# Four transposes of two-byte data moved from TensorE to transposing DMAs on SyncE, in a decoder layer on one core

## The reference, cut to what matters

```
1. x = LN(x + [x + rec + bit_linear(silu(bit_linear(rms(rec), w_gate)), w_down)])
     with h = rms(x); a = sigmoid(bit_linear(h, w_a) + bias); i, v alike;
     rec[t] = a[t] * rec[t-1] + sqrt(1 - a^2) * i * v          (a scan over tokens)
     bit_linear(h, w): each token of h is scaled to +-127 and rounded, w is rounded to -1, 0, 1
2. x = LN(x + attention(x, ctx))      16 heads of 16, rotary embedding, softmax over 256 keys
3. x = LN(x + s2 * relu2(s1 * relu2(s0 * [x, -x] @ k0) @ k1) @ k2)      k entries are +-1
```

## Time and profile before

| | |
|---|---|
| median of three runs | 956.42 us |
| profiled execution | 957.39 us, of which 955.6 us are the span from the first to the last instruction |
| PE busy | 832.9 us (87%) |
| DVE busy | 689.7 us (72%) |
| ACT busy | 544.1 us (57%) |
| POOL busy | 300.1 us (31%) |
| chain that ended last | PE 47%, DVE 22%, DMA 10%, ACT 9%, issue 7% |
| granted TensorE clock | mean 0.97, full in nearly all of the span after the first tenth |

### The profile page before, as it was taken

The page is one execution under the profiler, slowest core; times in us unless marked ns, Lnnn a source line. Parts: engine busy times, 40 slices in busy tenths (PEclk is TensorE's granted clock), DMA queues, the critical chain, the costliest instruction groups (busy, mean ns, idle before and its releaser), DMA issues.

```text
span 955.6 us, 17622 instructions
## 1 busy us (share of the span) xinstructions
PE 832.9 (87%) x6750; PEld 629.4 (66%) x6750; DVE 689.7 (72%) x1249; ACT 544.1 (57%) x909; POOL 300.1 (31%) x483
## 2 busy tenths in 40 slices
PE   1557789999999999999989999999999999997876
PEld 1233457786777777686867677676867677775655
DVE  8566578686969787786869696886869697866332
ACT  2453756657484747657574747566574747472331
POOL 5331415142423315151433334051424334141001
PEclk9876799999999999999999999999999999999999
DMA  8033160707052441707061532607070524325000
GB/s 277 0 59 53 45 79 16 108 13 117 8 101 34 71 64 41 94 13 122 14 106 17 90 46 52 83 27 108 14 114 10 101 34 62 62 38 75 1 12 22
DMA packets 98323, 57.43 MB, mean 60 GB/s; under 512 B 7841, under 2 KB 97473, under 8 KB 98241
## 3 DMA queue, kind: packets, MB, share of 16 engines
q1 hardware_dynamic: 98240, 56.31, 35.7%
HBM read 39.24 MB, written 16.79 MB: 59 GB/s over the span
## 4 chain that ended last, share of the span: by engine, by line
PE 47%; DVE 22%; DMA 10%; ACT 9%; issue 7%; POOL 2%; SPq 2%; DVEq 0%; ACTq 0%; POOLq 0%
PE bankC L1006 12%; PE bankA L816 11%; PE bankC L991 6%; DMA out<-x 6%; PE bankA L942 5%; PE slotB L910 3%; PE slotB L929 3%; PE bankA L807 3%; DMA q_st<-m_lo 3%; DVE x L1234 3%; DVE bn L1226 2%; DVE st L1204 2%; DVE nmax L1283 2%; ACT L666 2%; POOL rstd L534 2%
## 5 line engine op out<-in xcount | busy, mean ns | idle before, releaser
L1006 PE MATMUL bankC<-h0h,w 128*128 128x256 f16 x1024 | 233.4, 273 | 6.7 <-DVE h0l L1327 6.7
L1006 PE MATMUL bankC<-h0l,w 128*128 128x256 f16 x1024 | 232.9, 273 | 0.0
L1283 DVE TENSOR_REDUCE nmax<-slotB 128x4 f32<-128x1024 f32 x128 | 153.2, 1218 | 7.5 <-PE slotB L910 6.7
L716 ACT ACTIVATE pr<-slotB 128x1024 f32<-128x1024 f32 x128 | 129.3, 1025 | 37.6 <-PE slotB L929 37.4
L1006 PEld LDWEIGHTS bankC<-h0h,w 128*128 128x128 f16 x1024 | 100.5, 98 | 22.7 <-issue 9.8
L1006 PEld LDWEIGHTS bankC<-h0l,w 128*128 128x128 f16 x1024 | 100.4, 98 | 11.9
L533 POOL TENSOR_SCALAR rstd<-mv 128x2 f32<-128x2 f32 x48 | 9.3, 193 | 295.6 <-DVE mv L1229 295.6
L910 PE MATMUL slotB<-k_st,q_st 97*128 97x256 bf16 x512 | 78.9, 279 | 8.1 <-issue 5.1
L929 PE MATMUL slotB<-q_st,k_st 99*128 99x256 bf16 x512 | 75.9, 276 | 8.4 <-DMA q_st<-m_lo 4.8
L498 POOL TENSOR_SCALAR st<-st 128x2 f32<-128x2 f32 x32 | 7.7, 240 | 230.9 <-ACT junk L658 194.1
L1327 DVE SCALAR_TENSOR_TENSOR h1l<-bankC,h1h 128x512 f16<-128x512 f32 x64 | 43.6, 682 | 41.9 <-ACT h1h L741 41.9
(11 more groups left out here) (197 smaller groups left out, 1789.5 us busy)
## 6 DMA issues: line engine op xcount, KB each, us to landing
k_st<-scr SPq DMA_DIRECT2D x96, 128.0 KB, 5.2
q_st<-scr SPq DMA_DIRECT2D x96, 128.0 KB, 4.9
scr<-kpart SPq DMA_DIRECT2D x16, 384.0 KB, 3.6
scr<-qpart SPq DMA_DIRECT2D x16, 384.0 KB, 3.7
x<-in_x SPq DMA_DIRECT2D x16, 256.0 KB, 2.9
cT<-in_ctxT SPq DMA_DIRECT2D x16, 256.0 KB, 2.9
out<-x SPq DMA_DIRECT2D x16, 256.0 KB, 5.3
pr<-in_k SPq DMA_DIRECT2D x1, 1024.0 KB, 10.2
```

The source lines that it names most:

```text
L716: act.activation(pr[i % 2][:, c, :, :].rearrange("p h s -> p (h s)"), slotB[ringB.slot(g, name)][:, :], ACT.Exp, scale=DH ** -0.5).then_in ...
L1006: ins = pe.matmul(bankC[ringC.slot(g, name)][:, e * T:(e + 1) * T], w_1[:, i // 2, (2 * m + e) * P:(2 * m + e + 1) * P], (h0h, h0l)[i % 2] ...
L1283: dve.tensor_reduce(nmax[:, hg * HG * NT + n:(hg + 1) * HG * NT:NT], slotB[ringB.slot(g, name)][:, :].rearrange("p (h s) -> p h s", s=S), ...
```

## The change: what it does

For `xqT`, `rqT` and the gate, DVE's `round_tokens` gets one more pass: it takes `ROUND` off again and writes a bf16 copy (`xq`, `rq`, `gq`) with tokens on partitions. For `x2`, ACT and DVE now form the high and the low part before the transpose, side by side in one tile `x2p`. Then SP issues one transposing DMA each, SBUF to SBUF: `xqT` and `rqT` move 128 KB (four 128x128 blocks of two-byte numbers), the gate (`sqT`) and `x2T` 256 KB (eight blocks). PE's transposes for these, ACT's drains with `neg_round` and the PSUM slots of all four are gone. The projections wait for the DMA's semaphore and read the tile by token block. POOL's `scale` now waits for `round2` of the group before, and `gate` on ACT for its `round3`, since both reuse a source tile.

```diff
+            def across(src, dst, arrived):
+                sp.dma_start_transpose(dst, src).then_inc(arrived.sem, 16)
...
+            def sqT_(g):
+                if g >= 1:
+                    sp.wait_ge(*ringA.filled(g - 1, "down"))
+                sp.wait_ge(*q3.at(g))
+                across(flat(gq), sqT[:, :, :, :].rearrange("p n c t -> p (n c) t"), sqT_in)
+
+            def x2T_(g):
+                if g >= 1:
+                    sp.wait_ge(*ringC.filled(g - 1, f"l0_{KT // 2 - 1}"))
+                sp.wait_ge(*xl_s.at(g))
+                across(x2p[:, :, :, :].rearrange("p a n d -> p (a n d)"),
+                       x2T[:, :, :, :, :].rearrange("p a n c t -> p (a n c) t"), x2T_in)
...
-            def unround(g, name, dst):
-                act.wait_ge(*ringA.filled(g, name))
-                act.activation(dst, bankA[ringA.slot(g, name)][:, :], ACT.Identity, bias=neg_round)\
-                   .then_inc(ringA.free_sem(g, name), 1)
...
-            def sqT_(g, k):
-                if k == 0:
-                    pe.wait_ge(*q3.at(g))
-                transposed(g, f"sqT{k}", sg[:, :, 2 * k * P:(2 * k + 2) * P])
...
-            def round_tokens(g, src, factor, done):
+            def round_tokens(g, src, factor, dst, gone, done):
                 for n in range(NT):
-                    ins = dve.tensor_scalar(src[:, n, :], src[:, n, :], factor[:, n:n + 1], ROUND, ALU.mult, ALU.add)
-                ins.then_inc(done.sem, 1)
+                    own.mark(dve.tensor_scalar(src[:, n, :], src[:, n, :], factor[:, n:n + 1], ROUND, ALU.mult, ALU.add))
+                own.settle()
+                if g >= 1:
+                    dve.wait_ge(*gone.at(g - 1))
+                dve.tensor_scalar(dst[:, :, :], src[:, :, :], -ROUND, None, ALU.add).then_inc(done.sem, 1)
...
-                dve.tensor_tensor(flat(xl), slotB[ringB.slot(g, "x2T")][:, 0:512], flat(xh), ALU.subtract)\
-                   .then_inc(ringB.free_sem(g, "x2T"), 1)
+                dve.tensor_tensor(x2p[:, 1], x2[g % 2][:, :, :], x2p[:, 0], ALU.subtract).then_inc(xl_s.sem, 1)
```

More of the change, by code:

```diff
@@ L52 @@
 TIMES = """
[L53 to L72, removed]
@@ L73 @@
-    l1_3.0 P169.46 | l1_3.1 P171.66 | l1_3.2 P173.27 | l1_3.3 P173.89 A182.97 V185.57 | l2.0 P184.84 | l2.1 P190.11
-    l2.2 P190.5 | l2.3 P192.35 V196.85 | bn3 V233.28 G247.94 | out A239.18 | store S228.22
+    w:s V-358.73 P-345.58 | w:m V-255.03 A-334.52 P-294.13 | w:a V8.56 | w:iv V27.56 | w:g1 V8.92 P-141.16
+    w:g2 V21.1 A4.94 P17.85 | w:gate V32.32 | w:down V46.74 | w:bv P16.86 A27.81 | w:bias P39.65 V67.73
+    w:mask V23.89 S22.86 | w:sgn V32.42 | w:k0 V49.53 | w:k2 V60.27 | w:k1.0 A46.61 | w:k1.1 A66.03 | w:k1.2 A101.24
@@ new lines @@
+    w:k1.3 A112.84 | w:rbk G27.13 | loadx S75.98 | loadc S133.66 | scale A0 G5.04 V3.65 | stat1 G17.5 | round V9.79
+    xqT S18.34 | iv0 P29.33 A30.86 V33.66 | iv1 P31.53 A33.54 V32.75 | a P14.91 A23.29 | aT P27.95 A29.67
+    sq A33.67 | ivT P36.5 V34.38 | cum V34.64 | recur V37.33 | rec P42.81 A41.36 V44.61 | max2 V44.95 | stat2 G46.07
+    round2 V45.93 | rqT S64.43 | gate0 P54.85 A53.74 V54.83 | gate1 P55.41 A57.91 V56.09 | stat3 G58.47
+    round3 V56.51 | sqT S70.13 | down P61.75 V63.26 | bn V65.59 G77.42 | x1 V72.53 | kv0 P39.4 A40.55
@@ new lines @@
+    kv1 P41.46 A52.41 | rotk G52.22 | krT P58.53 A59.58 V62.77 G73.84 | kput S70.68 | kget S71.73
+    x1T P64.24 A71.82 | xb G92.01 | q P64.9 V78.72 | rotq G87.46 V80.29 | qrT P79.22 A81.89 V81.33 | qput S89.05
+    qget S95.74 | score0 P95.11 V92.1 | score1 P95.72 V94.03 | score2 P97.32 V97.13 | score3 P98.97 V97.95
+    score4 P100.72 V102.44 | score5 P104.92 V103.12 | score6 P107.79 V103.73 | score7 P108.58 V106.7
+    max P110.48 A111.55 V109.12 | maxrow S122.37 | exp0.0 P112.75 A114.43 | exp0.1 P112.95 A114.63 | pv0 P116.67
@@ new lines @@
+    exp1.0 P114.08 A114.91 | exp1.1 P115.58 A116.83 | pv1 P117.18 A126.19 | exp2.0 P116.79 A116.99
+    exp2.1 P117.13 A123.31 | pv2 P119.99 | exp3.0 P117.84 A126.73 | exp3.1 P117.9 A129.42 | pv3 P122.17 A134.14
+    oTok P124.27 V133.79 | oT P135.45 A135.88 | wo P136.57 V137.96 | bn2 V138.37 G151.09 | x2 V140.72
+    x2T A144.38 V141.09 S169.48 | l0_0 P150.05 A152.72 V147.7 | l0_1 P150.24 A155.3 V149.72
+    l0_2 P150.69 A156.08 V150.65 | l0_3 P151.12 A156.1 V150.9 | l1_0.0 P154.42 | l1_0.1 P154.57 | l1_0.2 P156.73
@@ L97, in order @@
     return [(step, g) for _, _, step, g in sorted(steps)]
-A_ITEMS = {"xqT": ("ACT", "xqT"), "iv0": ("DVE", "iv0"), "iv1": ("DVE", "iv1"), "a": ("ACT", "a"),
-           "aT": ("ACT", "aT"), "ivT": ("DVE", "ivT"), "rec": ("DVE", "rec"), "rqT": ("ACT", "rqT"),
-           "gate0": ("ACT", "gate0"), "gate1": ("ACT", "gate1"), "sqT0": ("ACT", "sqT0"), "sqT1": ("ACT", "sqT1"),
+A_ITEMS = {"iv0": ("DVE", "iv0"), "iv1": ("DVE", "iv1"), "a": ("ACT", "a"),
+           "aT": ("ACT", "aT"), "ivT": ("DVE", "ivT"), "rec": ("DVE", "rec"),
+           "gate0": ("ACT", "gate0"), "gate1": ("ACT", "gate1"),
            "down": ("DVE", "down"), "kv0": ("ACT", "kv0"), "kv1": ("ACT", "kv1"), "x1T": ("ACT", "x1T"),
@@ L108 @@
            **{f"exp{i}.{c}": ("ACT", f"exp{i}.{c}") for i in range(NHG) for c in range(NT)},
-           "oTok": ("DVE", "oTok"), "oT": ("ACT", "oT"), "wo": ("DVE", "wo"), "x2T": ("DVE", "x2T")}
+           "oTok": ("DVE", "oTok"), "oT": ("ACT", "oT"), "wo": ("DVE", "wo")}
 C_ITEMS = {**{f"l0_{m}": ("DVE", f"l0_{m}") for m in range(KT // 2)},
@@ L449, in _ @@
             steps = {"w:mask": mask_row, "loadx": later(loadx), "loadc": later(loadc), "kput": kput, "kget": kget,
-                     "qput": qput, "qget": qget, "maxrow": maxrow, "store": store}
+                     "qput": qput, "qget": qget, "maxrow": maxrow, "store": store, "xqT": xqT_, "rqT": rqT_, "sqT": sqT_, "x2T": x2T_}
             for step, g in order("SP"):
@@ L667, in gate @@
                                scale=st[g % 2][:, 15, n:n + 1]).then_inc(ringA.free_sem(g, f"gate{n}"), 1)
-            def sqT_(g, k):
-                if k == 0 and g >= 1:
-                    act.wait_ge(*ringA.filled(g - 1, "down"))
-                unround(g, f"sqT{k}", flat(sqT[:, 2 * k:2 * k + 2, :]))
             def kv(g, n):
@@ L872, in down_ @@
                     pe.wait_ge(gd_s, 2)
[L873 to L875 removed]
+                pe.wait_ge(*sqT_in.at(g))
+                projected(g, "down", w_down, (0, D), by_tile(sqT), KG, [0, 1])
             def kv_(g, n):
```

112 lines of the change are left out of this document (61 added, 51 removed).

## The result

The changed kernel takes 984.1 us, the median of 4 runs from 980.8 to 987.4, against 957.3 us for the kernel before, now the median of four. The ratio is 1.026, with a 95% interval of 1.019 to 1.033. It is slower. The forecast was 969 us, with 933 to 1040 as its range: the sign is right, the size falls short by 15 us. The profiled execution took 986.15 us, of which the span is 984.4; before, 957.4 and 955.6.

What follows compares the result with a forecast made beforehand. It took the chain of waits, not PE, as the bound. Per group -0.85 + 0.3 + 0.9 = +0.35 us, +5 over 13 groups, plus 3 and 5 at the ends, on 957.4: 970, stated as 969 us, range 933 to 1040.

Steps and rivals of the forecast that it cites:

- Rival 1: PE is the bound after all, so its 2.2 us leave each period: 934 us, faster; chance 0.28.
- The four pieces: One group's period cut at four points on the chain of waits: 53.50 us before, 52.65 forecast without DMA costs.
- the two DMA prices: Waits for transposing DMAs in each group: 0.3 us for the gate's `sqT`, 0.9 us for `x2T`.
- A: From `m_lo` to the start of `x1T`: 10.67 us before, 11.5 forecast without DMA cost, 0.8 more.
- D: From `score0` to the next `m_lo`: 18.25 us before, 19.1 forecast without DMA cost, 0.85 more.
- B: From the start of `x1T` to the end of `pv3`, PE full: 6.72 us before, 6.15 forecast, 0.6 less.
- C: From the end of `pv3` to `score0`: 17.86 us before, 15.9 forecast, 2.0 less.
- the floor: In C, the queries' write and read back allow `score0` no sooner than 16.2 us after `pv3`, whatever PE does.
- the meeting of `round2`: In D, `round2`'s new DVE pass comes as POOL starts `rotk` and is held up: 1.2 us charged a group.
- Rivals 3 and 4: Transposing DMAs go by the piece, 6.5 us: 1036 us, chance 0.16; or block after block, 14.8 us: near 1255, chance 0.04.
- rival 4: DMAs turn block after block, 14.8 us: `sqT` 11, `x2T` 9.9, some 20 us a group, near 1255 us; chance 0.04.
- The ends: Filling and draining add whole DMA latencies: +5 us in the first group (`rqT`, `sqT`), +3 in the last (`x2T`).

Runs made afterwards that it cites:

- the version of 960.9 us: The changed kernel with POOL's `xb` moved ahead of `rotq` and x2 turned by PE again: 960.9 us, ratio 1.001 to the kernel before.
- the three that take as long as the kernel before: Changed kernel with `xb` early and x2 on PE (960.9 us); that with layer 0's and 2's weights prepared later (957.1); that again with rq on PE (959.4).
- the version of 957.1 us: The version of 960.9 us with layer 0's and layer 2's weights prepared later on DVE: 957.1 us, ratio 0.997 to the kernel before.

## Why the prediction was half right

**What bounds the kernel: right.** PE's busy share went from 94% to 90.5% and the period did not shrink. Rival 1 (934 us) would have had 50.9 us a group; no kernel that was run came below 52.85.

**The four pieces.** In the group from 490.02 to 543.25, which has no fall, with the two DMA prices put where they were charged (A and D):

- A: 11.8 forecast, 11.89 measured.
- B: 6.15 forecast, 5.87 measured.
- C: 15.9 forecast, 17.35 measured.
- D: 20.0 forecast, 18.13 measured.

The sum is 53.85 forecast and 53.24 measured. The good sum hides two misses of opposite sign.

**C missed by 1.45 us, and this is the step that failed.** It has two faults of about the same size.

The first is the floor. The prediction took the end of the read back from the DMA share, 0.99 until 505.20, and concluded that PE came to `score0` later for reasons of its own. But the sixth read of that group, issued at 500.35, takes 6.5 us to land:

```profile
q_st<-scr SPq DMA_DIRECT2D x1, 128.0 KB, 6.5
```

That is 506.81, and `score0` starts at 506.90. In each of the eleven middle groups of the kernel before it starts 0.09 us after the last landing, as in the changed kernel. So C was bound by the queries from the start, and its floor in the kernel before is 17.9 us, not 16.2: from the first issue to the last landing 8.7 us pass on average, before and after the change, where 7.2 were counted. What the change gains in C is that `qput` lands 2.8 us after its issue instead of 4.0.

The second is the meeting. The prediction took `qput`'s chain as it stood, less one drain, and did not ask what POOL does beside its links. It looked for new meetings of DVE and POOL in A and in `round2`, credited 1.1 us because `xb` would no longer meet `round` or `x1`, and did not look where `xb` went: behind `rotq`, onto `qt`, 1.0 us on the path of the queries. `qput` goes out 5.7 us after `pv3`, and 5.0 with `xb` early.

Over the eleven middle groups C is 17.9 us on average in the kernel before, 17.3 in the changed one and 16.6 with `xb` early, for a forecast of 15.9. So 0.7 us of the miss is the meeting and 0.7 the floor.

**D: the meeting of `round2` didn't take place.** The prediction charged 1.2 us. The pass is at 536.28, POOL's `rotk` at 537.52, because in the new order it has to wait for ACT:

```profile
536.28 0.43 DVE L1164 TENSOR_SCALAR rq<-xg 128x512 bf16<-128x512 f32 x1
...
537.52 1.27 POOL L586 TENSOR_TENSOR kt<-kb,rope 128x512 f32<-128x512 f32 x1 [1.22 <-ACT v_aug L709]
```

Without this 1.2 and without the 0.9 for `x2T`, which wasn't paid either (below), the forecast of D is 17.9. The mechanism was right, as the passes alone in the old order show (1.53 us); the place was wrong, since only POOL's due time was compared, and not the wait before it.

**The DMAs.** `sqT` lands in 3.1 us where 4.1 was forecast, and still is on the chain in every group, 3% of the span. The price of 0.3 us fits A's 11.89. `x2T` is issued 12.3 us after C begins and lands 5.8 later, at 18.1 us; 12.3 and 18.15 (15.9 + 2.25) were forecast. Its 0.9 us a group wasn't paid: with `xb` early, the middle with x2 on the DMA is 52.85 us, on PE 52.95. Rivals 3 and 4, DMAs by the piece or block after block, are refuted by 3.1 us for eight blocks. In the sum of rival 4 there is a slip: 14.8 us in place of 4.1 makes its `x2T` term 11.6 and not 9.9.

**The clock was not in the sum at all.** Behind a wait of PE it forecast only the wait. Six falls cost 2.1 us each, 12.6 us, which is all of the middle's 11.6 and a little more. So the middle's +1.06 us a group instead of +0.35 has another cause than any term of the sum: PE's slack in C, made longer by the change and by the meeting. Without the falls it would be 53.1 against 53.19, no loss at all. Where the prediction wrote that "the chain gives back little of PE's 2.2 us", their loss took something away: 0.86 us of useless work put in there gained 7 us.

**The ends: 8 forecast, 17 measured.** What `x2T` costs in the drain is sized about rightly: after the last `m_lo` x2 on PE saves 3.9 us (58.8 us against 62.7, with `xb` early in both), 3 were forecast. The drain as a whole is no longer than before (62.7 against 62.6), because the new order makes the rest of it shorter, which was not forecast. Its chain in the changed kernel:

```profile
946.98 3.06 DMA x2T<-x2p
950.08 6.07 PE bankC L1005 x32
```

Where the first entry has landed, PE takes 6.07 us for 32 matmuls; 32 of the same size take 3.65 us in the middle of the version of 960.9 us, and the granted clock of 950 to 954 us is 0.50: a fall is in this price as well. In the filling 3.5 us of the excess are the weights' conversions, not a transposing DMA. The rest of the ends is in every version of the new order that was run: in the three that take as long as the kernel before, 1.6 to 3.4 us in the first two groups and 3.9 to 5.5 in the last two. In the changed kernel the clock has a part in it: its mean is 0.94 in the first two and in the last two groups, 0.98 in both before, and in the last group PE waits 5.55 us for `score0`, where before it did not wait. But the version of 957.1 us has 0.98 in its last two groups as well and still takes 3.9 us more there, so the cause of the rest stays open.

**The chances.** Slower had 0.60, and slower came. The size was not that of a rival either: 12 of the 29 us come from the clock behind PE's slack, 17 from the ends. That slower came is in part luck: the forecast had 5 us for the steady groups by terms of which the larger ones (1.2 and 0.9 us a group) were not paid, and without the falls a middle group is as long as before.

## What to carry to other kernels

Work taken off an engine that isn't last turns into waits, and on PE a longer wait can cost more than itself: look at the granted clock of each stretch behind PE's longest wait, and keep other work standing inside it. When an order is written anew, check each two-input or pass-through operation of DVE against what POOL runs at that time, by POOL's real start (its wait included), on the critical chain first. When a floor is read from a DMA, take the landing of its last transfer and not the end of the busy share, here 1.6 us apart. A transposing DMA can be worth more than the engine time it saves, by the place it frees in an in-order engine: here 2.5 to 5.2 us a group for the gate, against the two places that were tried.

## What the runs showed of the hardware

- A transposing DMA from SBUF to SBUF lands in 2.4 us (`rqT`) for 128x512 two-byte numbers and in 3.1 us (`sqT`) for 128x1024, and holds SP for 1.2 us or more at its issue. Behind six reads of 128 KB each the larger one took 5.8.
- Six reads of 128 KB land 8.7 us after the first is issued, although the mean share of the DMA engines is already down 1.6 us earlier (0.08 between 505.20 and 506.90 in the kernel before).
- DVE's `tensor_tensor` of two SBUF operands, 128x512 f32, takes 0.69 us alone and 1.68 when a `tensor_tensor` of POOL of 1.27 us is running. The Trainium skill ("SBUF — State Buffer", Who interferes with whom) counts DVE operations with two SBUF inputs among those that the lock concerns; the trace agrees.
- PE's granted clock fell to the level of 1.2 GHz behind six of the eleven waits of the changed kernel, for most of the next 4 us. These six were 1.81 to 2.24 us long, the other five 1.25 to 1.86. With the gate on PE a wait of 2.53 passed without a fall, and a fall also came behind two waits of 0.97 and 0.84 us that stood close together. No row tells what decides.
